# A new order of four engines for the third stage of a fused attention and gated-MLP kernel, `down` three tiles behind, x normalised in place

## The chip, the cores and the metric

The kernel runs on one core of a Trainium2 chip. A core has TensorE (PE, matmuls and transposes), VectorE (DVE), ScalarE (ACT), GpSimd (POOL) and SyncE (SP, which issues the DMAs here); they run their own instruction streams and meet through semaphores. The metric is the device time of one execution in microseconds.

## What is computed

The input x is 2 x 1024 tokens of 512 numbers, float32. The reference, cut to what matters:

```python
xn = _layernorm(x)                       # mean and variance over the 512
# s: attention, 32 heads of 16, q and k layer-normed, ALiBi, causal softmax
qkv = clip(xn @ Wqkv.T, -8, 8);  q, k = ln(q), ln(k)
o = softmax(q k^T * 0.25 + slope * rel, causal) v
s = o @ Wout.T
# g: gated MLP, 512 -> 1792 -> 512, 4-bit weights (w - zero) * scale, groups of 128
gate = silu(xn @ gate_w);  up = xn @ up_w
g = silu((gate * up) @ down_w)
return x + s * g
```

## The kernel before

Three stages follow one another, with a barrier between them. The first normalises x, projects q, k and v and stores them; the second does the attention and at the same time unpacks the MLP weights into `w_gu` and `w_d`, and leaves the heads' output in `o_sb`. Both are untouched. **The third stage**, which the change is about, does the projection of `o_sb` by `Wout`, the MLP and the residual.

It goes over the tokens in four blocks (`b`, `NB` = 4) of 512. Inside a block it goes over the 1792 hidden units in 14 tiles (`it`, `IT` = 14) of 128. Large operands are split in two float32r parts, hi and lo, and both are multiplied. For a tile:

- TensorE, `gate_up` (lines 1465, 1466): eight pairs of matmuls j = 0 to 7, each `xc_lo` then `xc_hi` with one 128x128 weight. Even j is gate, odd j up, k = j // 2 the group of 128 inputs, each with its own scale. The four PSUM banks `GB[j % 4]` (in the two tensors `pair`) take them in turn.
- ScalarE, `first` (L1223): j = 0 and 1, scaled, into `gate` and `up` buffers (`acc`; the second up buffer is `sg0`, shown as sg). VectorE, `add` (L1339): j = 2 to 7, scaled and added.
- ScalarE, `silu` (L1227) on gate; VectorE, `gate` (L1346): gate times up, in place, called the product below; ScalarE, `h_high` (L1197), `h_hi`; GpSimd, `h_low` (L1157), `h_lo`, the rest of the product.
- TensorE, `down` (L1475, L1476): for each of four output groups t one pair of matmuls with `h_lo` and `h_hi` into a bank `y[t]`. For t = 0, 1, 2 ScalarE, `copy_down` (L1250), scales it into one of three `tmp` buffers (`oin_v` is one of them) and GpSimd, `add_down` (L1167), adds it to `yt[t]`; for t = 3, and for all four in the last tile, VectorE does both in `sum_down` (L1354). In tile 0 ScalarE writes `yt` itself.

Around the tiles of a block: VectorE's `norm` (L1317) writes normalised x into `xnc`, TensorE's `trans_x` (L1428) transposes it, ScalarE's `hi_x` and VectorE's `lo_x` (L1327) make `xc_hi` and `xc_lo`; `trans_o`, `hi_o`, `lo_o` (L1322), `s_project` (L1447) and `copy_s` make s of the block in `s_sb`; and for the block before, `trans_y` (L1437), `silu_y` (L1254), `mul_y` (L1359) and `add_x` (L1176) finish g, s times g, and the residual. SyncE loads x into `xin_c` twice a block, once for the norm and once for the residual (`load_x`), and stores the result.

The order of the work is written out by hand for each engine; each engine does its list in order, and a wait in it holds up all that is behind it. Before the change `down` runs two tiles behind `gate_up`, and there are three `h` buffers, two gate buffers and two up buffers.

## Time and profile before

| | us |
|---|---|
| median of 3 runs | 1170.83 (1167.23 to 1180.91) |
| the profiled execution | 1172.41 |
| its span | 1170.5 |
| PE busy in the span | 1071.2 (92%), 6242 matmuls |
| DVE busy | 926.3 (79%) |
| ACT busy | 725.2 (62%) |
| POOL busy | 465.0 (40%) |
| mean granted TensorE clock | 0.993 |

The third stage takes 715 to 1170 us of the span. A matmul's record lasts longer than the distance to the next one, since matmuls are pipelined, so that a busy share of TensorE overstates it; where the pace matters, the distance of two starts is read. Other records overlap the next one a little too, VectorE's adds by 0.08 us. Where idle time is given in brackets, it is that of the engine just before the instruction, with what ended it.

### The profile page before, as it was taken

What the parts mean: (1) busy time and instruction counts of PE and PEld (TensorE: products, weight loads), DVE (VectorE), ACT (ScalarE), POOL (GpSimd) and SP (SyncE); (2) the same over time, 40 slices, a digit from 0 to 9 for tenths busy, and PEclk for the clock granted to TensorE, in tenths of its full rate; (3) what the DMA queues carried; (4) which work ended last, traced back from release to release, by engine and by line L of the source; (5) the groups of instructions that cost most, each with busy time, mean ns of one, the idle gap of its engine ahead of it and who ended that gap; (6) DMA issues with size and microseconds to landing.
All of it is one profiled execution on the core that took longest, in us unless ns stands there. A gap on an engine that the chain in (4) does not pass through costs nothing. (4 is left out here: it accounts for less than half of the span.)

```text
span 1170.5 us, 19003 instructions
## 1 busy us (share of the span) xinstructions
PE 1071.2 (92%) x6242; PEld 631.1 (54%) x6242; DVE 926.3 (79%) x2147; ACT 725.2 (62%) x1167; POOL 465.0 (40%) x554
## 2 busy tenths in 40 slices
PE   6999888999999999999999998999899889989995
PEld 4788764333333333333333335766676677667663
DVE  6788797888887888888887854589768977996886
ACT  3666545766766666766766675466556646654663
POOL 2666544111212021111212020278547835872786
PEclk9999998999999999999999999999999999999998
DMA  5345644343433344343434331000200120012001
GB/s 205 95 137 173 186 109 152 96 119 93 122 91 104 104 136 104 91 122 87 122 92 106 101 102 38 0 1 28 74 8 1 37 73 1 1 36 72 1 1 37
DMA packets 98585, 95.33 MB, mean 81 GB/s; under 512 B 28030, under 2 KB 80950, under 8 KB 98486
## 3 DMA queue, kind: packets, MB, share of 16 engines
q1 hardware_dynamic: 96854, 93.72, 28.1%
q8 instruction: 50, 0.82, 0.3%
q10 hardware_dynamic: 1632, 0.39, 0.2%
q14 instruction: 49, 0.40, 0.1%
HBM read 72.45 MB, written 21.23 MB: 80 GB/s over the span
## 5 line engine op out<-in xcount | busy, mean ns | idle before, releaser
L885 ACT ACTIVATE pr<-pair 128x1024 f32<-128x1024 f32 (+3 forms) x384 | 293.2, 811 | 150.5 <-PE pair L1001 97.0
L268 DVE CUSTOM_DVE_ANT_0 bank<-bank,sg 128x384 f32<-128x384 f32 (+1 forms) x488 | 227.6, 522 | 64.4 <-PE bank L278 61.0
L1465 PE MATMUL pair<-xc_lo,w_gu 128*128 128x512 f32 x448 | 185.7, 415 | 9.0 <-DVE gate L1339 3.6
L1466 PE MATMUL pair<-xc_hi,w_gu 128*128 128x512 f32 x448 | 176.5, 394 | 0.0
L1339 DVE SCALAR_TENSOR_TENSOR gate<-pair,sgu,gate 128x512 f32<-128x512 f32 x168 | 124.7, 742 | 58.7 <-PE pair L1466 51.7
L271 DVE TENSOR_REDUCE mx<-bank 128x1 f32<-128x512 f32 x240 | 150.2, 683 | 8.9 <-PE bank L278 8.2
L1157 POOL TENSOR_TENSOR h_lo<-gate,h_hi 128x512 fp32r<-128x512 f32 x56 | 72.1, 1288 | 158.0 <-ACT h_hi L1197 158.0
L1167 POOL TENSOR_TENSOR yt<-yt,tmp 128x512 f32<-128x512 f32 x96 | 124.9, 1323 | 0.0
L1465 PEld LDWEIGHTS pair<-xc_lo,w_gu 128*128 128x128 f32 x448 | 84.6, 189 | 54.2 <-DVE gate L1339 21.8
L278 PE MATMUL bank<-ks,qs 108*128 108x512 bf16 (+3 forms) x384 | 107.7, 329 | 5.3 <-DVE mx L268 5.1
L1475 PE MATMUL bank<-h_lo,w_d 128*128 128x512 f32 x224 | 95.0, 424 | 17.2 <-POOL h_lo L1157 12.5
L278 PE MATMUL bank<-xin_c,s_sb 108*128 108x512 bf16 (+3 forms) x344 | 97.6, 332 | 4.4 <-DVE mx L268 4.1
L996 PE MATMUL pair<-s_sb,xin_c 111*128 111x512 bf16 (+3 forms) x384 | 94.3, 330 | 6.4 <-ACT dt L397 2.9
L996 PE MATMUL pair<-qs,ks 111*128 111x512 bf16 (+3 forms) x384 | 93.1, 327 | 7.6 <-ACT pr L885 4.2
L1197 ACT ACTIVATE h_hi<-gate 128x512 fp32r<-128x512 f32 x56 | 35.4, 632 | 103.2 <-DVE gate L1346 103.2
L1466 PEld LDWEIGHTS pair<-xc_hi,w_gu 128*128 128x128 f32 x448 | 84.8, 189 | 14.9
L1476 PE MATMUL bank<-h_hi,w_d 128*128 128x512 f32 x224 | 88.5, 395 | 0.0
L852 POOL TENSOR_TENSOR w_gu<-sst,zst 128x896 fp32r<-128x896 f32 x16 | 33.3, 2084 | 135.6 <-ACT zst L898 122.7
L373 POOL TENSOR_SCALAR dneg<-mx 128x16 f32<-128x16 f32 x32 | 8.2, 255 | 197.1 <-DVE mx L268 112.2
L711 PE MATMUL bank<-wq_hi,xt_lo 128*128 128x512 f32 x192 | 80.0, 417 | 5.3 <-DVE xt_lo L599 5.3
L1011 PE MATMUL bank<-pr,oin_v 128*17 128x512 f32 (+3 forms) x768 | 80.6, 491 | 0.0
L1011 PE MATMUL bank<-pr,vs 128*17 128x512 f32 (+3 forms) x768 | 80.6, 491 | 0.0
(125 smaller groups left out, 2096.4 us busy)
## 6 DMA issues: line engine op xcount, KB each, us to landing
stk<-parts SPq DMA_DIRECT2D x16, 768.0 KB, 5.6
zst<-in_z_all SPq DMA_DIRECT2D x24, 448.0 KB, 4.1
sst<-in_w_all SPq DMA_DIRECT2D x24, 448.0 KB, 4.8
xin_c<-in_x SPq DMA_DIRECT2D x32, 256.0 KB, 3.1
s_sb<-stk SPq DMA_DIRECT2D x96, 64.0 KB
xin_c<-stk SPq DMA_DIRECT2D x96, 64.0 KB
qs<-stk SPq DMA_DIRECT2D x96, 64.0 KB
ks<-stk SPq DMA_DIRECT2D x96, 64.0 KB
```

What stands on the lines that cost most here:

```text
L268: dve.tensor_tensor_reduce(out=src, in0=src, in1=tri[:, 512 - w:512], scale=1.0, scalar=-3.0e38, op0=ALU.add, op1=ALU.max, accum_out=dst). ...
L271: dve.tensor_reduce(dst, src, AX.X, ALU.max).then_inc(m_free, 1)
L278: pe.matmul(b[:, 0:w], qs[s][0:ROWS_MAX, qt // 4, j, (qt % 4) * P:(qt % 4 + 1) * P], ks[s][0:ROWS_MAX, j, k0:k0 + w], start=True, stop=Tru ...
L885: act.activation(pr[e % 3][:, 2 * p:2 * p + 2, 0:w], pair[p][:, :, 0:w], ACT.Exp, scale=SCALE)\
L996: mm = pe.matmul(pair[p][:, jj, 0:512 - c0], ks[s][0:ROWS, j, kt * P:(kt + 1) * P], qs[s][0:ROWS, qb, j, c0:512], start=True, stop=not dia ...
L1011: mm = pe.matmul(b_o[32 * j:32 * j + VW, c0:512], vs[s][:, kt, j * VW:(j + 1) * VW], pr[e % 3][:, j, 0:512 - c0], start=(kt == 0), stop=(k ...
L1167: pool.tensor_tensor(yt[t][:, :], yt[t][:, :], tmp[n % 3], ALU.add).then_inc(dn_pool, 1)
L1339: dve.scalar_tensor_tensor(out=a, in0=GB[j % 4], scalar=scale_of(n, k, it), in1=a, op0=ALU.mult, op1=ALU.add)\
L1465: pe.matmul(GB[j % 4], w, xc_lo[:, k, :], start=True, stop=False)
L1466: pe.matmul(GB[j % 4], w, xc_hi[:, k, :], start=False, stop=True).then_inc(gu_done, 1)
L1475: pe.matmul(y[t][:, :], w_down(it, t), h_lo[it % 3][:, :], start=True, stop=False)
L1476: pe.matmul(y[t][:, :], w_down(it, t), h_hi[it % 3][:, :], start=False, stop=True).then_inc(dn_done, 1)
```

## The change

The lists of all four engines and of SyncE are written anew in the third stage. `down` runs three tiles behind. There are four `h_hi` and `h_lo` and three gate buffers, and buffers are counted over all tiles of all blocks (`m` or `n` = IT * b + it) and no longer from 0 in each block. `norm` writes in place into `xin_c` and the `xnc` buffers are gone; the four norms of the next block stand behind tile 3. `yt` now shares its place in memory with `of_hi` and `of_lo`, and `tmp` no longer does. The last tile's `down` of a block goes into tile 0 of the next one. The instructions of the first two stages and the number of operations of the third are as before.

```diff
-            yt = [sc(f"yt{n}", [P, 512], F32) for n in range(KT)]
-            acc = [[sc("gate0", [P, 512], F32), sc("gate1", [P, 512], F32)], [sc("up0", [P, 512], F32), sg0]]
-            h_hi = [sc(f"h_hi{n}", [P, 512], F32R) for n in range(3)]
-            xnc = [sc(f"xnc{n}", [P, D], F32) for n in range(2)]
+            acc = [[sc(f"gate{n}", [P, 512], F32) for n in range(3)], [sc("up0", [P, 512], F32), sg0]]
+            h_hi = [sc(f"h_hi{n}", [P, 512], F32R) for n in range(4)]
 ...
             with ExitStack() as c1:
-                xnc += [sb_in(c1)(f"xnc{n}", [P, D], F32) for n in (2, 3)]
-                tmp = [oin_v[:, 0:512]] + [sb_in(c1)(f"tmp{n}", [P, 512], F32)[:, :] for n in (1, 2)]
+                yt = [sb_in(c1)(f"yt{n}", [P, 512], F32) for n in range(KT)]
 ...
+                for u in range(4):
+                    sp.wait_ge(xc_tr, u + 1)
+                    load_x(sp, 1, u)
+                for b in range(NB - 1):
                     for u in range(4):
+                        sp.wait_ge(xc_tr, 4 * (b + 1) + u + 1)
+                        load_x(sp, b, u)
+                    for u in range(4):
+                        store(b, u)
+                        load_x(sp, min(b + 2, NB - 1), u)
 ...   # POOL, of a block
+                    add_down(b - 1, IT - 2, 2)
+                    add_x(b - 1, 0)
+                    h_low(b, 0)
+                    add_x(b - 1, 1)
+                    add_x(b - 1, 2)
+                    h_low(b, 1)
+                    add_x(b - 1, 3)
+                    h_low(b, 2)
+                    h_low(b, 3)
+                    for t in range(KT):
+                        add_down(b, 1, t)
+                    for it in range(5, IT):
+                        add_down(b, it - 3, 0)
                         h_low(b, it - 1)
+                        add_down(b, it - 3, 1)
+                        add_down(b, it - 3, 2)
 ...   # ACT
-                    if b > 0 or it > 1:
-                        act.wait_ge(hl_done, IT * b + it - 1)
+                    if n == 0 and m > 2:
+                        act.wait_ge(hl_done, m - 2)
+                    if n == 1 and m > 1:
+                        act.wait_ge(h_mul, m - 1)
 ...
+                    for it in range(5, IT):
+                        silu(b, it - 1)
+                        if it == 5:
+                            copy_down(b, 1, 2)
+                            copy_down(b, 1, 3)
+                        first(b, it, 0)
+                        first(b, it, 1)
+                        copy_down(b, it - 3, 0)
+                        h_high(b, it - 1)
+                        copy_down(b, it - 3, 1)
+                        copy_down(b, it - 3, 2)
 ...   # DVE
-                    dve.tensor_scalar(xnc[u][:, :], xin_c[:, u, :], xmean[:, t:t + 1], xrstd[:, t:t + 1],
+                    dve.tensor_scalar(xin_c[:, u, :], xin_c[:, u, :], xmean[:, t:t + 1], xrstd[:, t:t + 1],
 ...
+                    adds(b, 0, 2, 3)
+                    sum_down(b - 1, IT - 1, 0)
+                    adds(b, 0, 4, 7)
+                    sum_down(b - 1, IT - 1, 1)
+                    sum_down(b - 1, IT - 1, 2)
+                    sum_down(b - 1, IT - 1, 3)
 ...
+                    lo_o(b, 2)
+                    gate(b, 2)
+                    adds(b, 3, 2, 4)
+                    lo_o(b, 3)
+                    adds(b, 3, 5, 7)
+                    gate(b, 3)
                     if b < NB - 1:
                         for u in range(4):
+                            norm(b + 1, u)
+                    adds(b, 4, 2, 7)
+                    sum_down(b, 1, 3)
+                    for it in range(5, IT):
+                        gate(b, it - 1)
+                        adds(b, it, 2, 7)
+                        sum_down(b, it - 3, 3)
+                    gate(b, IT - 1)
 ...   # PE
+                    for t in range(4):
+                        gate_up(b, 0, t)
+                        down(b - 1, IT - 1, t)
 ...
+                    gate_up(b, 2, 0)
+                    trans_o(b, 0)
+                    gate_up(b, 2, 1)
+                    trans_o(b, 1)
+                    gate_up(b, 2, 2)
+                    s_project(b, 0, 0)
+                    gate_up(b, 2, 3)
+                    s_project(b, 0, 1)
+                    trans_o(b, 2)
 ...
+                    for it in range(5, IT):
                         for t in range(4):
                             gate_up(b, it, t)
-                            down(b, it - 2, t)
+                            down(b, it - 3, t)
+                    down(b, IT - 3, 0)
+                    if not last:
+                        trans_x(b + 1, 0)
+                        trans_x(b + 1, 1)
+                    down(b, IT - 3, 1)
 ...
```

What moves, at three places. First VectorE in an even stretch, tiles 6 and 7 of block 1, before (L1339 is `add`, L1354 `sum_down`, L1346 the product; pair0 and pair1 are the banks that TensorE wrote, gate0, up0, sg0 the buffers of a tile):

```order
L1339 SCALAR_TENSOR_TENSOR gate0<-pair1,sgu,gate0 128x512
L1339 SCALAR_TENSOR_TENSOR up0<-pair1,sgu,up0 128x512
L1354 SCALAR_TENSOR_TENSOR yt3<-bank3,oin_v,yt3 128x512
L1346 TENSOR_TENSOR gate1<-gate1,sg0 128x512
L1339 SCALAR_TENSOR_TENSOR gate0<-pair0,sgu,gate0 128x512
L1339 SCALAR_TENSOR_TENSOR up0<-pair0,sgu,up0 128x512
L1339 SCALAR_TENSOR_TENSOR gate0<-pair1,sgu,gate0 128x512
L1339 SCALAR_TENSOR_TENSOR up0<-pair1,sgu,up0 128x512
```

And with the change (L1375 is `add`, L1395 `sum_down`, L1387 the product):

```order
L1387 TENSOR_TENSOR gate1<-gate1,sg0 128x512
L1375 SCALAR_TENSOR_TENSOR gate2<-pair1,sgu,gate2 128x512
L1375 SCALAR_TENSOR_TENSOR up0<-pair1,sgu,up0 128x512
L1375 SCALAR_TENSOR_TENSOR gate2<-pair0,sgu,gate2 128x512
L1375 SCALAR_TENSOR_TENSOR up0<-pair0,sgu,up0 128x512
L1375 SCALAR_TENSOR_TENSOR gate2<-pair1,sgu,gate2 128x512
L1375 SCALAR_TENSOR_TENSOR up0<-pair1,sgu,up0 128x512
L1395 SCALAR_TENSOR_TENSOR yt3<-bank3,oin_v,yt3 128x512
L1387 TENSOR_TENSOR gate2<-gate2,up0 128x512
```

The y sum and the product of the tile before stood behind the first two adds of a tile; now the product stands ahead of all six adds and the sum behind them.

Second TensorE from block 0 to block 1, before (L1475 and L1476 are `down`, L1428 the transposes of x; two rows of `down` and tile 0's first `gate_up` come next):

```order
L1475 MATMUL bank3<-h_lo0,w_d 128x512
L1476 MATMUL bank3<-h_hi0,w_d 128x512
L1428 MATMUL pair0<-ident,xnc0 128x128 x4
L1428 MATMUL pair0<-ident,xnc1 128x128 x4
L1428 MATMUL pair1<-ident,xnc2 128x128 x4
L1428 MATMUL pair1<-ident,xnc3 128x128 x4
L1475 MATMUL bank0<-h_lo1,w_d 128x512
L1476 MATMUL bank0<-h_hi1,w_d 128x512
L1475 MATMUL bank1<-h_lo1,w_d 128x512
L1476 MATMUL bank1<-h_hi1,w_d 128x512
L1475 MATMUL bank2<-h_lo1,w_d 128x512
L1476 MATMUL bank2<-h_hi1,w_d 128x512
```

And with the change (L1540 and L1541, L1527 and L1528), from tile 12's `down` for group 2 on:

```order
L1540 MATMUL bank2<-h_lo0,w_d 128x512
L1541 MATMUL bank2<-h_hi0,w_d 128x512
L1540 MATMUL bank3<-h_lo0,w_d 128x512
L1541 MATMUL bank3<-h_hi0,w_d 128x512
L1527 MATMUL pair0<-xc_lo,w_gu 128x512
L1528 MATMUL pair0<-xc_hi,w_gu 128x512
L1527 MATMUL pair0<-xc_lo,w_gu 128x512
L1528 MATMUL pair0<-xc_hi,w_gu 128x512
L1540 MATMUL bank0<-h_lo1,w_d 128x512
L1541 MATMUL bank0<-h_hi1,w_d 128x512
L1527 MATMUL pair1<-xc_lo,w_gu 128x512
L1528 MATMUL pair1<-xc_hi,w_gu 128x512
```

The transposes of x stood between tile 12's `down` and tile 13's; tile 13's `down` now follows the first two pairs of the next block, one output group at a time, and the transposes stand five to seven pairs of `down` further up.

Third VectorE at the same hand-over, before (L1327 is `lo_x`):

```order
L1317 TENSOR_SCALAR xnc3<-xin_c,xmean,xrstd 128x512
L1354 SCALAR_TENSOR_TENSOR yt3<-bank3,mx1,yt3 128x512
L1346 TENSOR_TENSOR gate1<-gate1,sg0 128x512
L1354 SCALAR_TENSOR_TENSOR yt3<-bank3,mx1,yt3 128x512
L1327 TENSOR_TENSOR xc_lo<-pair0,xc_hi 128x4x128 x2
L1327 TENSOR_TENSOR xc_lo<-pair1,xc_hi 128x4x128 x2
L1354 SCALAR_TENSOR_TENSOR yt0<-bank0,mx1,yt0 128x512
L1354 SCALAR_TENSOR_TENSOR yt1<-bank1,mx1,yt1 128x512
L1354 SCALAR_TENSOR_TENSOR yt2<-bank2,mx1,yt2 128x512
L1354 SCALAR_TENSOR_TENSOR yt3<-bank3,mx1,yt3 128x512
L1339 SCALAR_TENSOR_TENSOR gate0<-pair1,sgu,gate0 128x512
L1339 SCALAR_TENSOR_TENSOR up0<-pair1,sgu,up0 128x512
```

And with the change (L1363 is `lo_x`):

```order
L1375 SCALAR_TENSOR_TENSOR sg0<-pair1,sgu,sg0 128x512
L1395 SCALAR_TENSOR_TENSOR yt3<-bank3,mx1,yt3 128x512
L1387 TENSOR_TENSOR gate0<-gate0,sg0 128x512
L1363 TENSOR_TENSOR xc_lo<-pair0,xc_hi 128x4x128
L1395 SCALAR_TENSOR_TENSOR yt3<-bank3,mx1,yt3 128x512
L1363 TENSOR_TENSOR xc_lo<-pair0,xc_hi 128x4x128
L1363 TENSOR_TENSOR xc_lo<-pair1,xc_hi 128x4x128 x2
L1395 SCALAR_TENSOR_TENSOR yt3<-bank3,mx1,yt3 128x512
L1375 SCALAR_TENSOR_TENSOR gate1<-pair1,sgu,gate1 128x512
L1375 SCALAR_TENSOR_TENSOR up0<-pair1,sgu,up0 128x512
L1395 SCALAR_TENSOR_TENSOR yt0<-bank0,mx1,yt0 128x512
L1375 SCALAR_TENSOR_TENSOR gate1<-pair0,sgu,gate1 128x512
```

The norm (L1317) is gone from here, and the four y sums of the last tile, which stood between `lo_x` and the block's first add, are now spread behind adds of tile 0.

## Rows read from the trace of the kernel before

**Rows 1.** Stretches: from:to, length, each engine's busy time (instructions), granted clock, DMA.

```profile
760.00:817.00 57.00, 55.33 (x216) 38.01 (x215) 52.89 (x75) 37.04 (x63) 45.38 (x36) 1.00 0.04 10
827.00:870.00 43.00, 39.79 (x182) 31.01 (x183) 29.22 (x45) 22.48 (x40) 15.22 (x13) 1.00 0.14 50
1158.00:1162.00 4.00, 3.06 (x12) 2.09 (x11) 3.00 (x4) 0.00 (x0) 1.33 (x2) 0.70 0.00 0
```

**Rows 2.** VectorE in time, an even tile: start, length, instruction, [idle before <-releaser].

```profile
871.76 0.74 DVE L1339 SCALAR_TENSOR_TENSOR gate<-pair,sgu,gate 128x512 f32<-128x512 f32 x1
...
875.16 0.75 DVE L1339 SCALAR_TENSOR_TENSOR gate<-pair,sgu,gate 128x512 f32<-128x512 f32 x1 [0.68 <-PE pair L1466]
...
876.49 0.74 DVE L1354 SCALAR_TENSOR_TENSOR yt<-bank,oin_v,yt 128x512 f32<-128x512 f32 x1
877.15 1.04 DVE L1346 TENSOR_TENSOR gate<-gate,up 128x512 f32<-128x512 f32 x1
878.11 0.74 DVE L1339 SCALAR_TENSOR_TENSOR gate<-pair,sgu,gate 128x512 f32<-128x512 f32 x1
```

**Rows 3.** TensorE in time: eight transposes, and around the same even tile.

```profile
832.36 1.03 PE L1437 MATMUL bank<-ident,yt 128*128 128x128 f32 x8
...
868.20 0.39 PE L1465 MATMUL pair<-xc_lo,w_gu 128*128 128x512 f32 x1
...
872.05 0.39 PE L1476 MATMUL bank<-h_hi,w_d 128*128 128x512 f32 x1
872.56 0.50 PE L1465 MATMUL pair<-xc_lo,w_gu 128*128 128x512 f32 x1
...
873.22 0.50 PE L1465 MATMUL pair<-xc_lo,w_gu 128*128 128x512 f32 x1
...
874.49 0.39 PE L1465 MATMUL pair<-xc_lo,w_gu 128*128 128x512 f32 x1
874.73 0.40 PE L1466 MATMUL pair<-xc_hi,w_gu 128*128 128x512 f32 x1
```

**Rows 4.** GpSimd in time: beside a product at 823.53, and in the even tile.

```profile
824.04 1.74 POOL L1167 TENSOR_TENSOR yt<-yt,oin_v 128x512 f32<-128x512 f32 x1
...
876.35 1.29 POOL L1167 TENSOR_TENSOR yt<-yt,oin_v 128x512 f32<-128x512 f32 x1
878.93 1.29 POOL L1157 TENSOR_TENSOR h_lo<-gate,h_hi 128x512 fp32r<-128x512 f32 x1 [1.29 <-ACT h_hi L1197]
```

**Rows 5.** VectorE in time: first norms, hand-over, first adds, an undisturbed product.

```profile
715.01 1.92 DVE L1317 TENSOR_SCALAR xnc<-xin_c,xmean,xrstd 128x512 f32<-128x512 f32 x4 [0.32 <-PEq L805]
...
823.53 1.10 DVE L1346 TENSOR_TENSOR gate<-gate,sg 128x512 f32<-128x512 f32 x1
...
826.97 2.48 DVE L1327 TENSOR_TENSOR xc_lo<-pair,xc_hi 128x512 fp32r<-128x512 f32 x4 [1.68 <-ACT xc_hi L1197]
829.37 2.72 DVE L1354 SCALAR_TENSOR_TENSOR yt<-bank,mx,yt 128x512 f32<-128x512 f32 x4
832.00 0.74 DVE L1339 SCALAR_TENSOR_TENSOR gate<-pair,sgu,gate 128x512 f32<-128x512 f32 x1
...
862.81 0.68 DVE L1346 TENSOR_TENSOR gate<-gate,up 128x512 f32<-128x512 f32 x1
...
926.50 0.74 DVE L1339 SCALAR_TENSOR_TENSOR gate<-pair,sgu,gate 128x512 f32<-128x512 f32 x1
...
942.15 0.74 DVE L1339 SCALAR_TENSOR_TENSOR gate<-pair,sgu,gate 128x512 f32<-128x512 f32 x1
```

**Rows 6.** ScalarE in time, in the even tile.

```profile
873.91 0.69 ACT L1223 ACTIVATE gate<-pair,sgu 128x512 f32<-128x512 f32 x1 [0.24 <-POOL h_lo L1157]
...
878.22 0.63 ACT L1197 ACTIVATE h_hi<-gate 128x512 fp32r<-128x512 f32 x1 [1.95 <-DVE gate L1346]
```

**Rows 7.** Tile xin_c in the third stage: norms (ns min/median/max), loads to landing.

```profile
L1317 DVE TENSOR_SCALAR xnc<-xin_c,xmean,xrstd x16: 540/1002/1018, 715.0 to 1042.3; 128x512 f32<-128x512 f32 x16
...
DMA to landing us min/median/max: 2.5/2.9/4.4
```

More of the change, by code:

```diff
@@ L1302, in _ @@
-                    if b < NB - 1:
-                        for u in range(4):
-                            hi_x(b + 1, u)
+                    first(b, 0, 0)
+                    first(b, 0, 1)
+                    copy_down(b - 1, IT - 2, 2)
+                    copy_down(b - 1, IT - 2, 3)
+                    silu(b, 0)
+                    first(b, 1, 0)
+                    first(b, 1, 1)
+                    if b > 0:
+                        for u in range(4):
+                            silu_y(b - 1, u)
@@ new lines, in _ @@
+                    copy_s(b, 2)
+                    silu(b, 3)
+                    h_high(b, 3)
+                    copy_s(b, 3)
+                    first(b, 4, 0)
+                    first(b, 4, 1)
+                    for t in range(KT):
+                        copy_down(b, 0, t)
+                    copy_down(b, 1, 0)
+                    copy_down(b, 1, 1)
+                    for it in range(5, IT):
[9 more added lines that the diff above has]
+                        copy_down(b, it - 3, 2)
+                        copy_down(b, it - 3, 3)
@@ L1357, in mul_y @@
                 def mul_y(b, u):
+                    if b < 0:
+                        return
                     dve.wait_ge(y_silu, 4 * b + u + 1)
```

315 lines of the change are left out of this document (145 added, 170 removed).

## The prediction, made before the changed kernel had run

> **What bounds the kernel now.** I read the stretches first. The changed stage runs from 715 us to the end of the span, four blocks long, and inside a block there are two kinds of stretch. In the even one (tiles 4 to 12) TensorE is busy 55.3 of 57 us and VectorE 52.9; in the first tiles of a block, where the attention projection is done, TensorE 39.8 of 43 and VectorE only 29.2 [rows 1]. TensorE is overstated by this: a matmul's record lasts 0.39 us, but seventeen steps between back-to-back ones take 868.20 to 872.05, 0.2265 us each [rows 3]; I use 0.228.
>
> A block's period is the distance of its first adds: 832.00 to 942.15, 110.15 us [rows 5]. It falls into tiles 0 to 4 (832.00 to 875.16, 43.2), tiles 5 to 12 (875.16 to 926.50, 51.3) and tile 13 with the hand-over (926.50 to 942.15, 15.6) [rows 2, 5].
>
> Now one even tile, 6.35 us long. VectorE starts the k=2 gate add at 871.76, ending at 872.50. That frees a PSUM bank: TensorE, idle, starts the next tile's first pair at 872.56, its second at 873.22 (held by the up add), does one `down`, and starts the k=1 gate pair at 874.49, done at 875.12 [rows 3]. VectorE waits 0.68 us for it, starts its k=1 add at 875.16, the other k=1 add, a y sum at 876.49, the gate product at 877.15, and only then the next k=2 add, at 878.11 [rows 2]. So **a ring through VectorE and TensorE** sets 6.35 us, while neither is full: VectorE has seven steps of 0.66 (two lie between 875.16 and 876.49) and a product of about 0.95, 5.6 us, TensorE 24 x 0.228 = 5.5. A second ring is as long: ScalarE waits for GpSimd's `h_lo` of two tiles back before it may overwrite the gate buffer (0.24 us), and GpSimd is idle 1.29 before `h_lo` [rows 4, 6].
>
> **The product is slowed by GpSimd.** Alone it takes 0.68 us (862.81); in the even stretch it starts at 877.15, GpSimd's add ends at 876.35 + 1.29 = 877.64, and the product ends 0.55 us behind that, at 878.19 [rows 2, 4, 5]. At 823.53 it ends at 824.63, and a GpSimd add started at 824.04 takes 1.74 instead of 1.29 [rows 4, 5]. So each waits for the other's whole instruction.
>
> **The change, part by part.**
>
> *Even tiles.* The product moves ahead of all six adds of the next tile, and the y sum behind them. Count from T, the k=1 gate add. Adds start at T, +0.66, ... +3.30, the sum at +3.96, the product at +4.62. The k=2 gate add (+1.32) ends at +2.06; TensorE's next k=0 pairs then start near +2.1 to +2.9 and, by the 3.40 us that lie between 871.76 and 875.16 now, its k=1 gate pair is done near 1.32 + 3.40 = +4.72, ahead of the product's end. VectorE's 0.68 wait is gone. What is late next: the product needs silu, which can start at +3.4 (end of the k=3 gate add) and takes 0.63 as h_hi does [rows 6]: +4.1, early by half a microsecond. The second ring opens too: three gate buffers let ScalarE run a tile further, and with `down` three tiles behind, `h_lo` has a whole tile of slack. ScalarE issues seven operations a tile of 0.69 us or less, under 4.9; GpSimd four of 1.29, 5.2.
> So VectorE sets the tile: 7 x 0.66 + the product. Free, the product costs 0.64 (5.26, then TensorE's 5.5 would bind); if it meets a GpSimd add with r us to go, it costs r + 0.47. GpSimd is busy 5.2 of 5.7 us; with r anywhere between 0 and 1.29 that is 0.49 more in nine of ten cases, 1.08 in the mean, so 5.7 a tile; the worst is 1.29 + 0.47, 6.4 a tile. I take 5.7. Eight tiles: 51.3 becomes 45.6.
>
> *Norms.* They leave tiles 10 to 13, where most take 1.0 us beside GpSimd [rows 7], and follow tile 3's product in a row. Four without GpSimd take 1.92 us [rows 5]. There GpSimd has one `h_lo` and the projections keep TensorE behind; I put the four at 2 to 3.7 us, in a stretch where VectorE has room. Their x must be there: its reload lands 2.9 us (up to 4.4) after its issue [rows 7], and the issue now follows the residual add and the store of the block before, which sit in tiles 1 to 3, the last one behind `h_lo` of tile 1. In-place writing needs no extra copy and no further DMA: 28 loads in both orders.
>
> *Tiles 0 to 4.* Here TensorE binds if its waits go, since the new order spreads the projection's matmuls over two tiles instead of one and a half, each between pairs of gate and up, and puts the last tile's four `down` between tile 0's pairs. Its work: 5 x 16 for gate and up, 8 x 3 for tiles 13, 0 and 1, 48 for the projection, 152 x 0.228 = 34.7; 32 transposes at about 0.11 (eight in 1.03, the record's tail in it [rows 3]) 3.5. Together 38.2. One wait stays: the y transposes need VectorE's last y sum, ten steps of 0.66 plus 0.74 behind its first add, about 1 us later than TensorE gets there; restarts behind waits cost 0.1 each (a record of 0.50 instead of 0.39 [rows 3]). I take 39.8, from 43.2. VectorE's own work there, 30 adds, 5 sums, 4 products, 8 small ones and the norms, is 33 to 36.
>
> *Hand-over.* Now VectorE waits 1.68 us for xc_hi, and does four y sums (2.72 us) between the last xc_lo and the first add [rows 5]. The transposes of x move five to seven pairs of `down` earlier, and those sums go into tile 0. Left for VectorE: six adds 4.0, three sums 2.0, one product 1.1, four xc_lo 2.4, and 1.7 from the last xc_lo to the first add's matmul: 11.2. TensorE's remainder is 40 x 0.228 + 16 x 0.11 = 10.9. I take 11.2, from 15.6.
>
> **Sum.** A block: 39.8 + 45.6 + 11.2 = 96.6, 13.5 less; three such hand-overs, 40.6. The last block has no norms and no hand-over: 3.4 + (8 x 6.35 - 45.6 = 5.2) = 8.6 less, and its drain is one tile of `down` longer, 8 x 0.228 = 1.8. Total 40.6 + 8.6 - 1.8 = 47.4 less. The profiled execution took 1172.4 us (span 1170.5), so 1125.0; the median of the runs shown is 1.6 lower. **I predict 1124 us.** Stages one and two keep their order. With free products (5.5 a tile, floor of TensorE) 32 tiles x 0.2 save another 6.4: 1117. With TensorE's waits in tiles 0 to 4 only halved, each block keeps 1.5 to 3 us: 1130 to 1136. The likeliest case's own range is 1115 to 1135.
>
> **Rivals.**
>
> *The product always meets GpSimd.* Now it meets it once a tile, at the same phase, because the whole tile is periodic. If it locks in just behind the start of an add each time, a tile is 6.4 us as now, the eight tiles save nothing, and 32 x 0.65 = 21 us of the gain stay out: 1145. For it: GpSimd will be nearly full (5.2 of 5.7). Against: the phase has to be the worst one, and a blocked product delays the `h_lo` that GpSimd waits for, which shifts the phase. The Trainium skill, SBUF — State Buffer, section "SBUF: two separate sides", calls the port pair that these two engines share an exclusive lock, in which "the other fully blocks"; the rows above agree, and by that rule GpSimd's denser queue speaks against this change. Chance 0.15.
>
> *TensorE's waits only move.* The first tiles hold chains over four engines (transpose, of_hi, of_lo, projection, copy, store). If one link is late in each of them, 3 to 4 us a block return and the hand-over saves half: 4 x 5 = 20, 1144. For it: VectorE now sits idle a third of that stretch [rows 1]. Against: more other matmuls now lie between the links. Chance 0.1.
>
> *Slower: the norm in the middle of a block.* It stands on VectorE's queue in front of all adds of tile 4, and its x is loaded only after store and residual add. Should the load be late, all four engines stand, and TensorE's granted clock falls with it (0.70 in 1158 to 1162, the halting end of the program [rows 1]). To be slower than before by 1% it would have to be late by (47 + 12) / 3 = 20 us in each of three blocks. Even the longest landing of 4.4 us leaves it in time by my count: residual add 3 is issued near 24 us into the block, its load lands near 28 to 30, the last norm is due near 31. So 1 or 2 us a block are possible, 20 hardly: 1185 if so. Chance 0.02.
>
> *The order is bound elsewhere and nothing moves* (within 1%, 1159 to 1182, about what a measurement can tell from no change): 0.03, as both rings would have to be misread.
>
> **Numbers.** Forecast 0.7, the rivals 0.15, 0.1, 0.02 and 0.03. The range 1112 to 1144 holds the forecast and about half of the first two rivals. Faster by over 1% 0.94, same 0.03, slower 0.03.
>
> **What would show it.** In the even stretch of the changed kernel: tiles 5.5 to 5.9 us apart; no wait of the k=1 gate add for TensorE; products of 0.7 to 1.7 us, and VectorE busy over 95%. `h_lo` no longer releases a gate activation. In the hand-over: no y sums between xc_lo and the first add, and 11 us from tile 13 to tile 0. In tiles 0 to 4 TensorE's matmuls back to back but for a wait ahead of the y transposes; norms at 0.5 to 1 us with no wait for a load. Wrong it would be if tiles stayed above 6.2 us, if VectorE waited for a DMA, or if the granted clock fell below 1.00 inside the blocks.

## The result and the profile after

| | before | after |
|---|---|---|
| median of 4 runs each, us | 1171.01 (1167.23 to 1180.91) | 1123.98 (1121.80 to 1124.50) |
| the profiled execution, us | 1172.41 | 1123.91 |
| its span, us | 1170.5 | 1121.8 |
| VectorE busy in the span, us | 926.3 | 926.4 |
| mean granted TensorE clock | 0.993 | 0.993 |

The ratio after to before is 0.9582, with a 95% interval of 0.9522 to 0.9642. The forecast was 1124. VectorE is as busy as before to a tenth of a microsecond; what went is waiting.

The distances of first adds say where. In block 1 of the changed kernel (814.15 to 911.68) a block lasts 97.53 us instead of 110.15: tiles 0 to 4 take 40.3 (before 43.2), tiles 5 to 12 take 46.0 (before 51.3), tile 13 with the hand-over 11.2 (before 15.6). Over the stage: blocks 0 to 2 give 15.3 + 12.6 + 12.4 = 40.3 us, the last block with its drain 5.8, and the stage's first add comes 2.5 us earlier, which is not the change: that add moved between 717.3 and 723.5 us from one kernel to another, though the first two stages were the same. The sum is the 48.7 us of the two spans. From the stage's first add to the end of the span it is 448.4 us before and 402.3 after: the change itself is worth 46.2.

The stretches of the changed kernel, in the columns of [rows 1]: block 1, its even part, the last block, and 4 us of the program's end.

```profile
814.15:911.68 97.53, 95.24 (x433) 75.79 (x432) 90.64 (x130) 65.46 (x113) 69.45 (x55) 1.00 0.10 33
851.00:900.00 49.00, 49.00 (x211) 38.48 (x210) 48.54 (x68) 35.97 (x62) 44.98 (x35) 1.00 0.00 1
1009.46:1121.80 112.34, 99.00 (x432) 77.66 (x430) 93.26 (x132) 65.41 (x111) 75.23 (x59) 0.96 0.09 29
1112.00:1116.00 4.00, 3.43 (x16) 3.03 (x16) 2.29 (x3) 2.28 (x4) 1.27 (x1) 0.57 0.00 0
```

VectorE is busy 48.54 of 49 us in the even part; the clock stays at 1.00 in the blocks and falls (0.57) only at the halting end.

VectorE in time, an even tile of the changed kernel, answering to [rows 2]:

```profile
865.45 0.94 DVE L1387 TENSOR_TENSOR gate<-gate,up 128x512 f32<-128x512 f32 x1
866.31 0.74 DVE L1375 SCALAR_TENSOR_TENSOR gate<-pair,sgu,gate 128x512 f32<-128x512 f32 x1
...
870.27 0.73 DVE L1395 SCALAR_TENSOR_TENSOR yt<-bank,oin_v,yt 128x512 f32<-128x512 f32 x1
870.93 1.37 DVE L1387 TENSOR_TENSOR gate<-gate,sg 128x512 f32<-128x512 f32 x1
872.22 0.74 DVE L1375 SCALAR_TENSOR_TENSOR gate<-pair,sgu,gate 128x512 f32<-128x512 f32 x1
```

GpSimd in time beside it, answering to [rows 4]:

```profile
863.29 2.55 POOL L1166 TENSOR_TENSOR yt<-yt,tmp 128x512 f32<-128x512 f32 x2
866.68 1.30 POOL L1166 TENSOR_TENSOR yt<-yt,oin_v 128x512 f32<-128x512 f32 x1 [0.84 <-ACT oin_v L1263]
...
869.20 2.54 POOL L1166 TENSOR_TENSOR yt<-yt,tmp 128x512 f32<-128x512 f32 x2
872.16 1.29 POOL L1166 TENSOR_TENSOR yt<-yt,oin_v 128x512 f32<-128x512 f32 x1 [0.42 <-ACT oin_v L1263]
```

No bracket stands on VectorE's rows: it waits for nobody. The product at 865.45 ends at 866.39, 0.55 us behind the GpSimd adds that end at 865.84; the one at 870.93 ends at 872.30, 0.56 behind those that end at 871.74. So tiles alternate, 5.47 us with a product of 0.94 and 5.91 with one of 1.37: the adds repeat at a period of two tiles, not of one.

The hand-over on VectorE, answering to [rows 5]:

```profile
905.06 1.37 DVE L1387 TENSOR_TENSOR gate<-gate,sg 128x512 f32<-128x512 f32 x1
906.35 0.68 DVE L1363 TENSOR_TENSOR xc_lo<-pair,xc_hi 128x512 fp32r<-128x512 f32 x1
...
907.61 1.87 DVE L1363 TENSOR_TENSOR xc_lo<-pair,xc_hi 128x512 fp32r<-128x512 f32 x3
909.41 0.73 DVE L1395 SCALAR_TENSOR_TENSOR yt<-bank,mx,yt 128x512 f32<-128x512 f32 x1
911.68 0.75 DVE L1375 SCALAR_TENSOR_TENSOR gate<-pair,sgu,gate 128x512 f32<-128x512 f32 x1 [1.54 <-PE pair L1528]
```

The 1.68 us of waiting for xc_hi is gone, and so are the four y sums before the first add: one sum and a wait of 1.54 for the first matmuls stand there.

The norms, on VectorE behind tile 3, and what follows them:

```profile
844.21 2.90 DVE L1353 TENSOR_SCALAR xin_c<-xin_c,xmean,xrstd 128x512 f32<-128x512 f32 x4
847.61 0.75 DVE L1375 SCALAR_TENSOR_TENSOR gate<-pair,sgu,gate 128x512 f32<-128x512 f32 x1 [0.50 <-PE pair L1528]
```

Four take 2.90 us, with no wait for a load. VectorE still waits for TensorE right behind them, so they cost nothing here.

The one stop of TensorE in the first tiles, in time:

```profile
820.97 0.63 PE L1499 MATMUL bank<-ident,yt 128*128 128x128 f32 x4 [1.33 <-DVE yt L1395]
```

Last, the waits of the whole third stage (who waited for whom, us in total, times, longest). Before:

```profile
POOL h_lo L1157 <- ACT h_hi L1197: 158.0, 52, 26.8
ACT h_hi L1197 <- DVE gate L1346: 103.2, 56, 3.0
DVE gate L1339 <- PE pair L1466: 51.7, 43, 3.7
PEld bank L1475 <- POOL h_lo L1157: 30.3, 44, 3.8
```

After:

```profile
POOL h_lo L1156 <- ACT h_hi L1209: 76.6, 12, 27.6
ACT gate L1241 <- DVE gate L1375: 73.2, 48, 3.6
...
DVE gate L1375 <- PE pair L1528: 24.1, 24, 3.3
...
ACT h_hi L1209 <- DVE gate L1387: 9.5, 24, 0.8
...
PEld bank L1540 <- POOL h_lo L1156: 2.6, 1, 2.6
```

VectorE's wait for a pair has halved; ScalarE waits 9.5 us for a product instead of 103, and waits now in front of silu (L1241), for VectorE's k=3 gate add; TensorE's weight load for `down` waited 30.3 us for `h_lo`, 44 times, and waits once now. The wait of a gate activation for `h_lo` [rows 6] has no row any more.

### The profile page after: what moved, and what is told of

It is laid out like the page before. It is cut to its first block and busy times, and to the rows that moved or that the text cites. A ratio compares the mean times of both kernels' runs of the same rounds, so it can differ in the third digit from the quotient of the medians.

```text
span 1121.8 us, 18965 instructions
## 1 busy us (share of the span) xinstructions
PE 1043.7 (93%) x6242; PEld 635.6 (57%) x6242; DVE 926.4 (83%) x2147; ACT 725.7 (65%) x1167; POOL 465.1 (41%) x554
## 5 line engine op out<-in xcount | busy, mean ns | idle before, releaser
L1527 PE MATMUL pair<-xc_lo,w_gu 128*128 128x512 f32 x448 | 181.5, 405 | 4.5 <-DVE xc_lo L1363 4.5
L1528 PE MATMUL pair<-xc_hi,w_gu 128*128 128x512 f32 x448 | 175.3, 391 | 0.0
L1375 DVE SCALAR_TENSOR_TENSOR gate<-pair,sgu,gate 128x512 f32<-128x512 f32 x168 | 124.5, 741 | 25.7 <-PE pair L1528 24.1
L1527 PEld LDWEIGHTS pair<-xc_lo,w_gu 128*128 128x128 f32 x448 | 84.1, 188 | 37.3 <-DVE up L1375 6.6
L1540 PE MATMUL bank<-h_lo,w_d 128*128 128x512 f32 x224 | 89.7, 400 | 2.9 <-POOL h_lo L1156 2.2
L1528 PEld LDWEIGHTS pair<-xc_hi,w_gu 128*128 128x128 f32 x448 | 84.3, 188 | 13.6
L1541 PE MATMUL bank<-h_hi,w_d 128*128 128x512 f32 x224 | 88.2, 394 | 0.0
L1241 ACT ACTIVATE gate<-gate 128x512 f32<-128x512 f32 x56 | 35.4, 632 | 73.2 <-DVE gate L1375 73.2
L1166 POOL TENSOR_TENSOR yt<-yt,oin_v 128x512 f32<-128x512 f32 x48 | 65.3, 1360 | 37.9 <-ACT oin_v L1263 37.5
```

The costliest lines, as they stand in the source:

```text
L1166: pool.tensor_tensor(yt[t][:, :], yt[t][:, :], tmp[n % 3], ALU.add).then_inc(dn_pool, 1)
L1375: dve.scalar_tensor_tensor(out=a, in0=GB[j % 4], scalar=scale_of(n, k, it), in1=a, op0=ALU.mult, op1=ALU.add)\
L1527: pe.matmul(GB[j % 4], w, xc_lo[:, k, :], start=True, stop=False)
L1528: pe.matmul(GB[j % 4], w, xc_hi[:, k, :], start=False, stop=True).then_inc(gu_done, 1)
L1540: pe.matmul(y[t][:, :], w_down(it, t), h_lo[n % 4][:, :], start=True, stop=False)
L1541: pe.matmul(y[t][:, :], w_down(it, t), h_hi[n % 4][:, :], start=False, stop=True).then_inc(dn_done, 1)
```

## The experiments

Below, "the changed kernel" and "before" name the two versions. Each kernel was compared with before on the same chip. Where two kernels are compared by their stage, it is the time from the third stage's first add to the end of the span, which leaves out the drift of that add.

**prod_third.** The changed kernel with the product back in third place, behind the first two adds of the next tile, from tile 5 on. Buffers, lag, norms and hand-over stay.

```diff
                     for it in range(5, IT):
+                        adds(b, it, 2, 3)
                         gate(b, it - 1)
-                        adds(b, it, 2, 7)
+                        adds(b, it, 4, 7)
```

> The changed kernel with the gate product of tiles 5 to 13 put behind the first two adds of the next tile, as it stood before the change; buffers, lag of down, norms and hand-over stay changed. Theory A (the product's place sets the even tile, by the ring through TensorE and by which GpSimd instruction it meets): the even tile goes back to 6.2 to 6.4 us from 5.48 and 5.91 in turn, the block from 97.5 to about 103.5, the time to about 1148 to 1151. Theory B (the deeper buffers and the longer lag of down gave the gain, the product's place gives nothing): even tile 5.7 as in the changed kernel, 1124.

Measured: 1150.11 us (1149.30 to 1152.94), ratio 0.9828 (0.9806 to 0.9851). Tiles are 6.35 us apart. VectorE in time:

```profile
873.70 1.69 DVE L1387 TENSOR_TENSOR gate<-gate,up 128x512 f32<-128x512 f32 x1
875.32 0.74 DVE L1375 SCALAR_TENSOR_TENSOR gate<-pair,sgu,gate 128x512 f32<-128x512 f32 x1
...
878.72 0.75 DVE L1375 SCALAR_TENSOR_TENSOR gate<-pair,sgu,gate 128x512 f32<-128x512 f32 x1
```

GpSimd, ScalarE and TensorE beside it:

```profile
873.54 1.31 POOL L1166 TENSOR_TENSOR yt<-yt,oin_v 128x512 f32<-128x512 f32 x1
876.13 1.29 POOL L1156 TENSOR_TENSOR h_lo<-gate,h_hi 128x512 fp32r<-128x512 f32 x1 [1.29 <-ACT h_hi L1209]
...
877.94 0.67 ACT L1236 ACTIVATE gate<-pair,sgu 128x512 f32<-128x512 f32 x1
...
878.02 0.40 PE L1529 MATMUL pair<-xc_hi,w_gu 128*128 128x512 f32 x1
```

The tile is 3.40 us from the k=2 gate add (875.32) to the next tile's k=1 gate add (878.72), and in between k=1 and k=2 two steps of 0.66 and the product's 1.62: 6.34. Before it was 3.40 + 3 x 0.66 + 0.96 [rows 2]: also 6.34. The 3.40 is the same number by another way. TensorE's pair for the k=1 gate add ends at 878.42, 0.30 us before the add starts, so its ring is open here. ScalarE's first activation ends at 878.61, and the add starts 0.10 us behind it, in all 24 tiles looked at to within 0.01; that activation stands behind silu, and silu waits for the k=3 gate add. But this ring holds VectorE up by only 0.10 us, since its own work in the tile is 7 x 0.66 + 1.62 = 6.24. So what fills the tile is the long product, and what buffers, lag and order opened went into it.

It is here, not in the changed kernel, that the meeting of the first rival comes true: GpSimd's add starts 0.16 us before the product, the product waits out nearly the whole of it, and this repeats in every tile. The rows show why it repeats. In this order h_hi, `h_lo` and two adds follow on the product one behind the other, and GpSimd's next add starts 4.5 us behind the product's end (873.54 behind 869.06). A longer product moves both alike and does not get them out of step.

**third_short.** Is the third place slow by itself, or only with GpSimd's adds in it? The same order, with each of GpSimd's sums of a `down` done on 32 of 512 columns.

```diff
# prod_third, and besides
-                    pool.tensor_tensor(yt[t][:, :], yt[t][:, :], tmp[n % 3], ALU.add).then_inc(dn_pool, 1)
+                    pool.tensor_tensor(yt[t][:, 0:32], yt[t][:, 0:32], tmp[n % 3][:, 0:32], ALU.add).then_inc(dn_pool, 1)
```

> The product in third place and GpSimd's adds on 32 columns (the rest of these sums left out). It splits theory A for the product's third place. If the ring through TensorE alone makes it slow, tiles stay above 6.0 us without GpSimd. If meeting a whole GpSimd instruction in each tile does (1.7 us a product), then without GpSimd's adds the tile falls to TensorE's 5.47 and the span to that of the kernel with short adds and the product ahead, within 2 us. From the distances in the trace I expect the second.

Measured: one run of 1115.35, span 1113.2. VectorE in time:

```profile
874.58 0.68 DVE L1387 TENSOR_TENSOR gate<-gate,sg 128x512 f32<-128x512 f32 x1
```

All products take 0.68 (0.60 to the add at 875.18), tiles are 5.44 apart. 3.40 + 2 x 0.66 + 0.60 is 5.32, so the ring is shorter than TensorE's 24 x 0.2265 = 5.44 and costs nothing. The third place is bad only by the product's length there, 1.62 instead of 0.60, once a tile; and a product of 1.62 would fill a tile of 6.24 on VectorE from any place. The place decides what the product meets.

**short_adds.** The changed kernel with that edit of `add_down` alone, to price the meeting that is left.

> The changed kernel with GpSimd's adds of down results on 32 of 512 columns (the other columns of these sums are left out), so that GpSimd hardly works beside VectorE. Theory A: no product waits, each is 0.68 to 0.72 us, tile 5.47 by TensorE, span 1109 to 1113 in all, of which the shorter end of the program is part. Rival (the product's length varies for another reason, such as ScalarE's or TensorE's traffic): products stay at 0.94 and 1.37, tile 5.7, span 1120.

Measured: one run of 1113.49, span 1111.4; products 0.68, tiles 5.44, a block 95.8. Against the changed kernel's 97.5 GpSimd costs 1.7 us a block. With the end of the program, which the short adds shorten too, it is 10.4 us of span, or about 13 of the stage. That tile is TensorE's.

**prod_second.** The product behind the first add of the next tile.

```diff
                     for it in range(5, IT):
+                        add(b, it, 2)
                         gate(b, it - 1)
-                        adds(b, it, 2, 7)
+                        adds(b, it, 3, 7)
```

> The changed kernel with the product of tiles 5 to 13 one place later, behind the first add of the next tile. In the changed kernel GpSimd is idle 0.4 and 0.85 us a tile just behind the product's start. Theory A: the product now starts in that gap, costs 0.7 us each time instead of 0.94 and 1.37, and the tile is bound by TensorE, 24 x 0.228 = 5.47: tile 5.47 us, 2 us less in all, 1121 to 1123. Theory A2 (only being ahead of the adds frees the ring, every place later costs): tile 5.9 or more, 1130. Theory B: 1124.

Measured: 1121.96 (1120.68 to 1123.68), ratio 0.9582 (0.9557 to 0.9607). GpSimd in time, beside a product at 873.12 of 0.82 us:

```profile
870.84 2.55 POOL L1166 TENSOR_TENSOR yt<-yt,tmp 128x512 f32<-128x512 f32 x2
873.59 1.51 POOL L1166 TENSOR_TENSOR yt<-yt,oin_v 128x512 f32<-128x512 f32 x1 [0.19 <-ACT oin_v L1263]
```

Tiles are 5.48 us apart, just above TensorE's 5.44 of short_adds; each k=1 gate add starts 0.10 us behind ScalarE's first activation, as in prod_third. The product ends 0.55 us behind the adds at 870.84, as ever, but they had little left to go; and the add behind it pays, 1.51 instead of 1.29. Tiles 5 to 12 take 44.6 instead of 46.0, but the hand-over takes 12.2 instead of 11.2: tile 12's product, a step of 0.74, now lies behind the first add of tile 13 and is counted here, and the last product meets an add for 1.57 us instead of 1.37. Median against median this is 2 us better than the changed kernel and by the stage 2.3, but the two ran on different chips, and their ratios to before are the same, 0.9582.

**old_prod_first.** The reverse: before, with nothing changed but the product's place, first from tile 4 on.

```diff
+                        if it >= 4:
+                            gate(b, it - 1)
                         add(b, it, 2)
 ...
-                        if it > 0:
+                        if 0 < it < 4:
                             gate(b, it - 1)
```

> The kernel before the change with one thing done: from tile 4 on the product of the tile before stands ahead of the first two adds (the y sum stays behind them); two gate buffers, three h buffers and down two tiles behind stay. Theory A (two rings of the same length): the ring through TensorE is cut, but silu comes only behind the two first evacuations and GpSimd's h_lo of two tiles back still holds the gate buffer, so the tile falls only from 6.35 to about 6.1 us, 36 tiles x 0.25 = 9 us, 1160 to 1164. If one ring alone counted (place of the product alone): tile 5.7, about 25 us less, 1145. If the deeper buffers alone counted: no change, 1171.

Measured: 1160.49 (1157.42 to 1161.43), ratio 0.9906 (0.9882 to 0.9931). VectorE in time:

```profile
871.23 0.74 DVE L1339 SCALAR_TENSOR_TENSOR gate<-pair,sgu,gate 128x512 f32<-128x512 f32 x1
...
874.75 0.69 DVE L1346 TENSOR_TENSOR gate<-gate,sg 128x512 f32<-128x512 f32 x1 [0.80 <-ACT gate L1227]
```

ScalarE beside it:

```profile
872.86 0.69 ACT L1223 ACTIVATE gate<-pair,sgu 128x512 f32<-128x512 f32 x1 [1.65 <-PE pair L1468]
873.51 0.69 ACT L1223 ACTIVATE up<-pair,sgu 128x512 f32<-128x512 f32 x1
874.10 0.62 ACT L1227 ACTIVATE gate<-gate 128x512 f32<-128x512 f32 x1
```

10 us instead of 47. Tiles are 6.11 apart: the product, now free of GpSimd, waits 0.80 us for silu. On ScalarE's old list silu stands behind the next tile's two first activations, these wait for TensorE's first pair, and that for the k=2 gate add at 871.23. So a ring through silu closes where the others open. The changed kernel is open there too, since its list has silu ahead of `first`.

**old_short.** Before, with the same edit of `add_down`.

> The kernel before the change with GpSimd's adds of down results on 32 of 512 columns (the rest of these sums left out). Of the 6.35 us of a tile the product's blocked part is on the ring (1.04 against 0.68 to 0.72): theory A expects 6.0 us a tile, 0.35 less, and since TensorE's wait and the late product stay, VectorE still idle in each tile; span 1150 to 1156. If contention with GpSimd were the main thing that held the old kernel, the tile would fall to 5.6 or less and the span to 1135.

Measured: one run of 1149.67, span 1147.8, a little under the 1150 to 1156 expected; products 0.68, tiles 6.00. GpSimd, TensorE, ScalarE and VectorE in time:

```profile
871.49 1.29 POOL L1157 TENSOR_TENSOR h_lo<-gate,h_hi 128x512 fp32r<-128x512 f32 x1 [1.97 <-ACT h_hi L1197]
...
872.84 0.51 PE L1475 MATMUL bank<-h_lo,w_d 128*128 128x512 f32 x1
...
872.82 0.69 ACT L1223 ACTIVATE gate<-pair,sgu 128x512 f32<-128x512 f32 x1 [0.25 <-POOL h_lo L1157]
...
874.07 0.75 DVE L1339 SCALAR_TENSOR_TENSOR gate<-pair,sgu,gate 128x512 f32<-128x512 f32 x1 [0.69 <-ACT up L1223]
```

`h_lo` ends at 872.78 and releases two engines: ScalarE's gate activation, and TensorE's `down` for this tile, 0.06 us later. The second is the one that counts. The gate activation is done at 873.51, 0.56 us before VectorE's k=1 gate add, where 0.10 is enough (prod_third). TensorE goes on from `down` to the k=1 gate pair, which ends at 874.04, 0.03 before the add. (The bracket names the up activation, but that one ends at 874.08, and this add doesn't need it.) Without the wait `down` would have followed at 872.69, a step behind the matmul at 872.46. So the ring that closes is product (870.07), h_hi (870.78), `h_lo`, `down`, gate pair, k=1 gate add, and with three steps of 0.66 the next product at 876.06: 5.99 us.

The kernel before has the same ring with a product 0.36 us longer, 6.35. There `h_lo` ends at 873.87 and this follows, where 873.79 would have been a step behind the matmul at 873.56:

```profile
873.93 0.50 PE L1475 MATMUL bank<-h_lo,w_d 128*128 128x512 f32 x1
```

In tiles 5 to 10 of block 1 `down` starts 0.05 to 0.06 us behind the end of `h_lo` each time. So 21 us of before were GpSimd's adds, the end of the program included, and a `down` only two tiles behind holds the tile at 6.0 even without them; the changed kernel without them reaches 5.44.

**old_sum_out.** Before, with the y sum taken out of the ring and put behind the six adds. If the ring through VectorE and TensorE were alone, 0.66 us a tile would go.

```diff
-                        elif it >= 4:
-                            sum_down(b, it - 3)
 ...
+                        if it >= 3:
+                            sum_down(b, it - 2)
```

> The kernel before the change with one thing done: from tile 3 on VectorE's y sum stands behind the six adds, of the tile whose down has just been done (two behind), so that it leaves the stretch between the k=1 and the k=2 adds. If the ring through TensorE were the only limit, the tile would fall by the sum's 0.66 to 5.7 us, 36 x 0.66 = 24 us, 1147. Mine: with two gate buffers and down two behind a second ring (gate buffer, first evacuation, product, h_hi, h_lo, gate buffer) is as long, GpSimd's instruction blocks the product longer instead, and the tile stays at 6.3 to 6.4 us: 1168 to 1175.

Measured: 1177.90 (1176.44 to 1179.29), ratio 1.0062 (1.0044 to 1.0080): 7 us worse, outside what I expected. VectorE in time:

```profile
888.96 1.70 DVE L1346 TENSOR_TENSOR gate<-gate,up 128x512 f32<-128x512 f32 x1
890.58 0.74 DVE L1339 SCALAR_TENSOR_TENSOR gate<-pair,sgu,gate 128x512 f32<-128x512 f32 x1
```

The tile stays at 6.35: the 0.66 that left the ring came back as product, 1.70 instead of 1.04. GpSimd's add starts at 888.82, 4.51 us behind the end of the product before (884.31). Before the change it is 4.51 too (876.35 behind 871.84), but the product then came 0.80 behind the add's start, and without the sum it comes 0.14 behind it. `down` starts 0.06 behind `h_lo` here too. Tiles 5 to 12 take 53.0 us instead of 51.3; what is over lies in the tiles with norms, 6.7 to 7.8 us apart.

**norm_late.** The changed kernel with the norms behind tiles 10 to 13, as before.

```diff
-                    if b < NB - 1:
-                        for u in range(4):
-                            norm(b + 1, u)
 ...
                         sum_down(b, it - 3, 3)
+                        if b < NB - 1 and it >= IT - 4:
+                            norm(b + 1, it - IT + 4)
```

> The changed kernel with the four norms of the next block put back behind tiles 10 to 13, one each. Mine: beside GpSimd a norm costs 0.9 us and VectorE binds there, while behind tile 3 four take 2.9 us where TensorE binds: 1.3 to 1.8 us a block more for three blocks, 1128 to 1130. Rival (the place of the norms is free, TensorE has slack): 1124.

Measured: 1131.90 (1130.76 to 1133.09), ratio 0.9667 (0.9645 to 0.9688), a little more than expected; by the stage it is 6.6 us more than the changed kernel. A block takes 99.5, 2.0 more, of which 0.7 in tiles 5 to 12, 1.1 at the hand-over and 0.2 ahead of them.

**handover_old.** The changed kernel with tile 13's `down` all ahead of the next block's first pairs, and its sums ahead of the first add.

```diff
-                    adds(b, 0, 2, 3)
-                    sum_down(b - 1, IT - 1, 0)
-                    adds(b, 0, 4, 7)
-                    sum_down(b - 1, IT - 1, 1)
-                    sum_down(b - 1, IT - 1, 2)
-                    sum_down(b - 1, IT - 1, 3)
+                    for t in range(KT):
+                        sum_down(b - 1, IT - 1, t)
+                    adds(b, 0, 2, 7)
 ...   # PE; on ACT the copies of tile 12 likewise ahead of first
-                        gate_up(b, 0, t)
                         down(b - 1, IT - 1, t)
+                    for t in range(4):
+                        gate_up(b, 0, t)
```

> The changed kernel with the hand-over of the blocks as before: TensorE does all four down of tile 13 ahead of the next block's first gate pair, ScalarE the last two copies ahead of its first evacuations, VectorE the four y sums ahead of the first add. Mine: VectorE's 2.7 us of sums and the wait for h_lo of tile 13 return to the path, tile 13 to tile 0 takes 16 us instead of 11.2, tiles 0 and 1 about 2 us less, in all 2.5 to 3 us a block: 1131 to 1133. Rival (the two places are equal, since TensorE has the same work): 1124.

Measured: 1133.73 (1130.44 to 1135.48), ratio 0.9683 (0.9651 to 0.9715), just above what was expected. VectorE in time:

```profile
915.94 0.75 DVE L1395 SCALAR_TENSOR_TENSOR yt<-bank,mx,yt 128x512 f32<-128x512 f32 x1 [2.50 <-POOL yt L1166]
917.18 0.75 DVE L1395 SCALAR_TENSOR_TENSOR yt<-bank,mx,yt 128x512 f32<-128x512 f32 x1 [0.49 <-POOL yt L1166]
```

The sums wait for GpSimd, whose list is that of the lag of three tiles, and the first add waits behind them. The hand-over takes 16.0 instead of 11.2; half of that comes back, as tiles 0 to 4 take 38.1 instead of 40.3. A block: 2.6 us.

**proj_packed.** The changed kernel with the attention projection in its old order, on TensorE's list alone. Its 48 matmuls lie between the same pairs of gate and up in both orders, from behind pair 2 of tile 2 to behind pair 3 of tile 3; what moves is that two transposes come later and the first matmuls come in twos.

```diff
+                    gate_up(b, 2, 1)
                     trans_o(b, 0)
-                    gate_up(b, 2, 1)
                     trans_o(b, 1)
                     gate_up(b, 2, 2)
                     s_project(b, 0, 0)
+                    s_project(b, 0, 1)
                     gate_up(b, 2, 3)
-                    s_project(b, 0, 1)
+                    s_project(b, 1, 0)
+                    s_project(b, 1, 1)
                     trans_o(b, 2)
                     gate_up(b, 3, 0)
-                    s_project(b, 1, 0)
+                    trans_o(b, 3)
+                    s_project(b, 2, 0)
 ...
```

> The changed kernel with the projection's matmuls spread as before the change (12 behind pair 2 of tile 2 and so on, one half at a time in tile 3), all else changed. Mine: TensorE again waits for of_lo and VectorE's adds, 3 us a block more, tiles 0 to 4 take 43 us instead of 40.3, 1134 to 1138. Rival (TensorE has the same work and the spread is free): 1124.

Measured: 1136.11 (1135.72 to 1137.76), ratio 0.9709 (0.9692 to 0.9725). TensorE in time:

```profile
841.49 0.50 PE L1509 MATMUL bank<-wo_hi,of_lo 128*128 128x512 f32 x1 [1.63 <-DVE of_lo L1358]
```

Another wait for of_lo, of 0.98, follows at 847.38. Tiles 0 to 4 take 43.5 instead of 40.3, about what they took before: the chain transpose, of_hi, of_lo, projection has too little other work between its links. The lists of ScalarE and VectorE, which hold of_hi and of_lo, stay those of the new order, so the run prices TensorE's order beside them and not by itself.

**best and changed_again.** `best` is prod_second with the first y transposes moved behind one more pair of tile 1; beside it ran the changed kernel once more.

```diff
# prod_second, and besides
                     gate_up(b, 1, 1)
-                    trans_y(b - 1, 0)
                     gate_up(b, 1, 2)
+                    trans_y(b - 1, 0)
```

> The changed kernel with two places moved: the product behind the next tile's first add in tiles 5 to 13, as in prod_second, and the first y transpose of the block before behind the third pair of tile 1 instead of the second, where TensorE waits for VectorE's last y sum. Mine: 0.5 to 0.8 us a block on top of prod_second, 1120 to 1122 against 1123 to 1125 for the changed kernel in the same call. Rival (the wait only moves to the next transpose): as prod_second, 1122.

> The changed kernel once more, on the same chip as best, to compare the two: 1122 to 1125.

Measured: best 1121.06 (1120.62 to 1121.77), ratio 0.9577 (0.9563 to 0.9591); the changed kernel 1124.70 (1124.28 to 1125.76), ratio 0.9609 (0.9595 to 0.9623), on the same chip. The runs touch nowhere: best is 3.6 us faster than the changed kernel. Its gain over prod_second, 1.5 us by the stage, lies inside the intervals of the two ratios; the blocks show it, as below. TensorE in time:

```profile
822.25 1.06 PE L1500 MATMUL bank<-ident,yt 128*128 128x128 f32 x8 [0.17 <-DVE yt L1395]
...
827.91 0.66 PE L1480 MATMUL bank<-ident,o_sb 128*128 128x128 f32 x4 [0.47 <-DVE s_sb L1402]
```

The wait of 1.33 us became 0.17, and 0.47 of the gain returned as a new wait further on; tiles 0 to 4 take 39.8 instead of the 40.3 of the changed kernel and of prod_second.

## Why the prediction was right

**The number.** That the time came out at the forecast to a tenth of a microsecond is luck. The sum said 47.4 us less; the spans gave 48.7, of which 2.5 are not the change. A block was to give 13.5: block 0 gave 15.3, the next two 12.6 and 12.4; the last, put at 6.8, gave 5.8.

**Even tiles.** Shown. The term was 5.7 us a tile out of seven steps of 0.66 and a product of 1.08 in the mean; measured are 5.69 and 5.69 - 7 x 0.66 = 1.07. The mean held, the reason for it only half: I spread the meeting over all phases, and it settled into two. With the product one and two places later the meeting settles into one phase each, and the tile takes 5.48 and 6.35 us; short adds bring the last to 5.44. So the place decides through what the product meets, and the first place is not the best one. Eight tiles took 46.0 against 45.6; what is over is the first, whose product took 1.80.

**The rings.** The kernel before was held by a ring, and a part of the prediction's account of it is wrong. It reads the first ring as k=2 gate add, PSUM bank, gate pair; `down` stands in between and waits for `h_lo`, so the ring that closes runs from the product over h_hi, `h_lo` and `down`. It exceeds the one by the bank alone by 0.14 us (873.93 instead of 873.79). The second ring, over the gate buffer, it calls as long; the gate activation was done 0.46 us earlier than needed, so that ring alone would give 5.89, an estimate from these rows. The change opened both, the ring over `down` by the lag of three tiles too, and not by the product's place alone. Whether the third gate buffer and the lag are each needed no run shows. A ring through silu showed in old_prod_first; the prediction counts silu early by half a microsecond without saying that this needs silu ahead of the next tile's `first`. The product alone out of its place gives 10 us, all the rest of the change without it gives 20 (prod_third, where hand-over and norms count too), both together 47.

**Hand-over.** 11.2 as forecast, 15.6 before, but with two errors that cancel: from the last xc_lo to the first add 1.7 us were counted and 2.2 measured, since a `down` pair stands in between, and one of the three sums counted falls into that wait. Undone the hand-over costs 2.6 us a block and not the 4.4 that the term says, as tiles 0 to 4 take the rest back. **Norms**: 2.90 us, inside 2 to 3.7; their old place costs 2.0 a block. **Tiles 0 to 4** came out at 40.3 against 39.8, and the wait ahead of the y transposes at 1.33 against about 1. TensorE's new order of the projection is worth 3.2 of them, beside the new lists of the other engines; it isn't spread over two tiles instead of one and a half, as the prediction says, but has its transposes earlier and its first matmuls one half at a time.

By the stage, the parts undone one by one cost 27.3 (product), 6.6 (norms), 7.5 (hand-over) and 12.4 us (projection). That is 53.8, more than the 46.2 of the whole: they share waits, so no single figure is "the" share of a part.

**Rivals.** The product that always meets GpSimd, priced at 6.4 us a tile, is a real state of this program, 6.35 in prod_third, but not of the changed kernel. The argument against it, that a blocked product delays `h_lo` and so shifts the phase, doesn't hold: in prod_third the delay moves GpSimd's adds along with the product and keeps the phase. In the changed kernel the phase alternates; GpSimd's first add there waits for ScalarE's copy (0.84 and 0.42 us) and not for anything behind the product. Why the first place escapes the one phase was not tried, and that the rival stayed away from it is in part luck: two places further down the list it is there. The Trainium skill, SBUF — State Buffer, section "SBUF: two separate sides", says that the loser of the shared port pair blocks for the winner's whole instruction; the runs agree (products of 1.70 us beside an add of 1.29, 0.68 in short_adds), but the page does not tell how often two engines meet, and that made the difference of 26 us between prod_third and the changed kernel. Late x, which would have made it slower, never showed: the loads land after 2.7 to 4.4 us, and the first norm starts without a bracket. TensorE's waits that only move were found in proj_packed, not here.

**Left open.** Why block 0 gained 15.3 us and the others 12.5. The difference lies in its tiles 0 and 1, which now take 9.3 us against 12.5 in block 1 (before 19.4 and 19.6). It has no block before it, and so no `down` of tile 13, no y transposes and no wait of 1.33 ahead of them, but that was not tried. In the last 15 us VectorE waits up to 3.9 us at a time for GpSimd's sums at a lag of three tiles:

```profile
1107.88 0.75 DVE L1395 SCALAR_TENSOR_TENSOR yt<-bank,mx,yt 128x512 f32<-128x512 f32 x1 [3.89 <-POOL yt L1166]
```

A shorter lag in the last block alone was not tried either.

## What to carry to other kernels

When no engine is full and the time is still flat, write down the ring: from an instruction to the same one a tile later, across the engines, and add up what stands inside it. Do it for each way round, down to the instruction that starts 0.03 to 0.10 us behind its releaser: here an inconspicuous `down` between two pairs closed the ring, the next ones were 0.14 and 0.46 us shorter, and one bracket named an instruction that ended too late to be the releaser. To move one operation pays only as far as the next ring. Where two engines exclude each other, look at the phase in which they meet before counting on a mean, and price a place by running it.

## What the runs showed of the hardware

- Product and GpSimd add, each 128x512 float32 with two SBUF inputs, alone 0.68 and 1.29 us. The product ends 0.55 us behind the add that it meets (0.94, 1.37, 1.57, up to 1.80); an add that starts while a product runs takes longer too, 1.51 in prod_second and 1.74 before [rows 4]. The six adds with a PSUM input kept their step of 0.66 beside GpSimd in every kernel.
- The meeting can lock: where an add starts 0.14 to 0.16 us before the product, and GpSimd's adds follow on the product of the tile before, it repeats in every tile (1.69 in prod_third, 1.70 in old_sum_out).
- VectorE's k=1 gate add starts 0.03 us behind the end of TensorE's pair where that releases it (before, old_short), and 0.10 behind ScalarE's activation where that one does (prod_third).
- A norm in place takes what one into another buffer takes, 0.53 and 0.54 us at the least.
- A first matmul behind a wait has a record of 0.50 us and a step of 0.34, the following ones 0.39 and 0.227 (841.49 and 841.83 in proj_packed).
